# Who normalises images 9 to 11, and who makes the first expert input: moving work between VectorE and GpSimd in the last rounds

## The chip, the cores and the metric

One core of a Trainium2 chip. The metric is the device time of one execution in microseconds (us), the median over runs.

## The reference

Sixteen images of 128 channels and 32 x 32 pixels pass through one block:

```
x = x + conv_attention(layernorm_over_channels(x))     # k softmax over pixels, context k.v, out = context.q, 1x1 conv
t = tokens(x)                                          # 1024 pixels as tokens of 128 channels
n = (t - mean) / sqrt(var + eps)                       # over the channels
w = softmax(mean_over_images(n) @ Wr + br)             # 8 experts, one weight per pixel and expert
t = t + sum_e w[:, e] * expert_e(n)                    # three layers of 128, batch norm and relu after the first two
```

The routing weights need the mean of n over all 16 images, so every expert product's weighting comes after all the attention.

## The kernel before, in words

It has two phases. The first is 16 rounds (t = 0 to 15), one image each, software-pipelined: in round t, TensorE makes the k products of image t, turns e and adds the G products of image t, finishes the output of image t-1 (heads_out, the m product, add_m), turns x1 of image t-2 into tokens, and the other engines normalise the tokens of image t-3 and add them to a running sum `feat` for the routing. The second phase is 128 slots (16 images x 8 experts), three layers each. A few expert products are slipped into round 15 and the tail between the phases; the first is `half_layer1(p_k, 0, 0)` in round 15, made from `xs_hi[0]` and `xs_lo[0]`.

Every engine runs its own program in the order written; semaphores tie them. Rounds 0 to 3 and 12 to 15 are written out, 4 to 11 are two turns of a loop. What matters of each engine in rounds 12 to 15:

- TensorE: k products (`k_half`, L583), `heads_out` (L506), turn of x1 (L564), turn of a coming x (only up to round 12), in round 15 `half_layer1` (L627), the y product (L460), three turns of e (`turn_e`, L597), `add_m` (L515 to L517), G products (`add_g`, L609) with the fourth turn of e, `turn_rows` (L526).
- ScalarE: `gT` (L800), `move_rows` (L890), two exponentials (`exp_half`, L916), copy of the turned x1 (L814), `mT_hi` (L818), `move_e` 0 and 1 (L906), `high_part` (xn_hi, L861), `move_e` 2 and 3, and its own norm chunks of image t-3 (`norm2_high`, L868; four of eight for images from 9 on, two before).
- VectorE: head maxima (L1145, L1148), `y_sb` (L1039), `statistics` (L1129 to L1139), `mT_lo` (L1058), bn_stats (L1109), the x1 sum (L1067), `xn_lo` (L1071), and in rounds 12 to 14 `norm2_part` (L1117).
- GpSimd: `scale_x` (L1368), `statistics` (pow, L1344; shift, L1351), then `norm2` (L1358, L1360) and `add_feature` (L1432).
- SP issues the DMAs in the order written: the store of `rows_out` (L334), the load of the broadcast row that scale_x multiplies by (L348), x, x1 scratch, and `load_rows` (L327), which waits for `xs_made`.

The ties that the text uses: `scale_x` waits for the row load and for the statistics; `high_part` waits for `scale_x`; `norm2_high` and `norm2` wait for the shift (`ln_done`); the row load waits for the store, which waits for `move_rows`, which stands behind `norm2_high` on ScalarE; `add_feature` waits for both halves of the chunks.

The first expert input is image 0's x1, read back into `xs_in[0]`, multiplied by one broadcast row (`scale_xs`), shifted by another (`shift_xs`), cast to `xs_hi[0]` (`first_xs_high`), and the remainder is `xs_lo[0]` (`split_low`).

Of the kernel before, what the change touches and what calls it, by code (L numbers as in the profile page):

```python
# [26 lines left out]
ALU = mybir.AluOpType  # L27
# [3 lines left out]
IMAGES, C, SIDE = 16, 128, 32  # L31
PIXELS = SIDE * SIDE
# [24 lines left out]
def at(t, n):  # L57

    return isinstance(t, int) and t == n


def metaformer_kernel(nc, x, w_qkv, w_out, b_out, Wr, br, W1, W2, Wo, small, bo, ident_in, heads_in, out):
# [25 lines left out]
    with ExitStack() as ctx:  # L88
# [700 lines left out]
        def _(act):  # L789
# [4 lines left out]
            def step(t, r, s, n, a, c, f, d):  # L794
                p = r % 2
                q = 1 - p
                if c:
                    act.wait_ge(g_done, t)
                    wait(act, y_done, t - 1)
                    nc.scalar.copy(gT[:], p_g[:, 0:LATENT]).then_inc(g_moved, 1)  # L800
                    move_rows(t, p, p_e)
                exp_half(t, p, 0)
                if at(t, 0):
                    move_rows(0, 0, p_e)
                exp_half(t, p, 1)
                if at(t, 0):
                    move_by_head(1)
                    copy_x(2, 2)
                if f:
                    act.wait_ge(x1t_done, t - 1)  # L810
                    wait(act, norm2_last, t - 3)
                    if at(t, 3):
                        act.wait_ge(w_split, 1)
                    nc.scalar.copy(x1_tokens[p], p_chan.rearrange("p (n c) -> p n c", c=C)).then_inc(copy2_done, 1)  # L814
                if c:
                    act.wait_ge(m_done, t)
                    wait(act, mx_done, t - 1)
                    nc.scalar.copy(mT_hi[:], p_g[:, 256:384]).then_inc(m_hi_done, 1)  # L818
                move_e(t, r, 0)
                move_e(t, r, 1)  # L820
                if s and not at(t, 0):
                    copy_x(t + 3, (r + 3) % 4)
                if at(t, IMAGES - 2):
                    first_xs_high(0)
                if at(t, IMAGES - 1):
                    h1_high(0, 0, p_k)
                if a and not at(t, 0):
                    high_part(t, (r + 1) % 4, q)
                move_e(t, r, 2)
                if at(t, IMAGES - 1):  # L830
                    norm2_high(t - 3, r, x1_tokens[q], xn2T)
                move_e(t, r, 3)
                if at(t, IMAGES - 1):
                    act.wait_ge(x1t_done, IMAGES - 1)
                    act.wait_ge(norm2_first, IMAGES - 3)
                    act.wait_ge(norm2_last, IMAGES - 3)
                    nc.scalar.copy(x1T[:], p_chan.rearrange("p (n c) -> p n c", c=C)).then_inc(copy2_done, 1)
                if at(t, 0):
                    high_part(t, (r + 1) % 4, q)
                    copy_x(3, 3)  # L840
                    act.wait_ge(expert_w, 6 * 16)
                    expert_weights_high(2)
                if at(t, 1):
                    act.wait_ge(w1_shifted, 1)
                    expert_weights_high(0)
                if at(t, 2):
                    act.wait_ge(scaled, 2)
                    expert_weights_high(1)
                if d and not at(t, IMAGES - 1):
                    norm2_high(t - 3, r, x1_tokens[q], xn2T)  # L850
# [34 lines left out]
            def move_rows(index, q, bank):  # L885

                act.wait_ge(rows_turned, index + 1)
                if not isinstance(index, int) or index >= 2:
                    act.wait_ge(rows_stored[q], stored_count(index, q) - 16)
                nc.scalar.activation(rows_out[q][:], bank[0:3 * CHUNKS, 384:512], ACT.Identity,  # L890
                                     bias=row_bias[:, 0:1]).then_inc(rows_moved, 1)

            def first_xs_high(b):

                act.wait_ge(xs_made, b + 1)
                nc.scalar.copy(xs_hi[b][:], xs_in[b][:]).then_inc(xs_hi_done, 1)
# [126 lines left out]
        def _(dve):  # L1023
            flat = [w_raw[:, k].rearrange("p e h -> p (e h)") for k in range(3)]

            def step(t, r, s, n, a, c, f, d):
                p = r % 2
                q = 1 - p
                for j in range(2):
                    head_max(t, j)  # L1030
                if c:

                    dve.wait_ge(exp_done, 2 * t)
                    nc.vector.reciprocal(rsum[:], sums[q][:]).then_inc(rsum_done, 1)
                    dve.wait_ge(rsum_done, t)
                    dve.wait_ge(y_done, t)
                    wait(dve, m_done, t - 1)
                    for j in range(2):
                        ins = nc.vector.tensor_scalar(y_sb[:, j, :], p_g[:, 128 * j:128 * (j + 1)], rsum[:, j:j + 1], None, ALU.mult)  # L1039
                    ins.then_inc(y_moved, 1)  # L1040
                if at(t, 0):
                    centre(0, 2, 2)
                    scale_weights(0)
                    halves(0, x_tokens[2], 2)
                if at(t, 1):
                    scale_weights(1)
                if n or at(t, IMAGES - 2):
                    statistics(t, slice(0 if n else 1, 2 if d else 1))
                if at(t, 0):

                    dve.wait_ge(wo_t2_done, 1)
                    nc.vector.tensor_tensor(bo_full[:], p_g[0:EXPERTS, 256:384], bo_sb[:], ALU.add).then_inc(bo_full_done, 1)
                    dve.wait_ge(shift_done, 1)
                    dve.wait_ge(scaled, 1)
                    nc.vector.tensor_tensor(flat[0], flat[0], p_chan, ALU.add).then_inc(w1_shifted, 1)
                if c:
                    dve.wait_ge(m_hi_done, t)
                    nc.vector.tensor_tensor(mT_lo[:], p_g[:, 256:384], mT_hi[:].bitcast(F32), ALU.subtract).then_inc(m_lo_done, 1)  # L1058
                if at(t, IMAGES - 1):
                    statistics(t, OF_X1)  # L1060
                if f:
                    halves(1, x1_tokens[p], t - 2)
                if c:

                    dve.wait_ge(mx_done, t)
                    dve.wait_ge(res_loaded[q], 8 * t + (0 if q else 8))
                    nc.vector.scalar_tensor_tensor(out=x_res[q][:], in0=p_chan, scalar=bout_sb[:, 0:1], in1=x_res[q][:],  # L1067
                                                   op0=ALU.add, op1=ALU.add).then_inc(x1_done, 1)
                if a:
                    dve.wait_ge(xn_hi_done, t + 2)  # L1070
                    nc.vector.tensor_tensor(xn_lo[q][:], x_in[(r + 1) % 4], xn_hi[q][:].bitcast(F32), ALU.subtract).then_inc(xn_lo_done, 1)  # L1071
                if s:
                    halves(0, x_tokens[(r + 3) % 4], t + 3)
                if isinstance(t, int) and IMAGES - 4 <= t < IMAGES - 1:
                    norm2_part(t - 3, r, x1_tokens[q], xn2T, range(4, CHUNKS), norm2_last)
                if at(t, IMAGES - 1):
                    statistics(IMAGES, OF_X1)
                    h1_low(0, 0, p_k)
# [212 lines left out]
        def _(pool):  # L1291
# [105 lines left out]

            def step(t, r, s, n, a, c, f, d):
                q = 1 - r % 2
                if at(t, 1):  # L1400
                    low_part(2, 1)
                if at(t, 2):
                    low_part(0, 2)
                if at(t, 3):
                    low_part(1, 3)
                if a:

                    pool.wait_ge(var_done, t + 3)
                    scale_x(t, (r + 1) % 4)
                if n or d:  # L1410
                    statistics(t, r, slice(0 if n else 1, 2 if d else 1))
                if at(t, IMAGES - 4):
                    scale_xs(0, 0)
                if at(t, IMAGES - 3):
                    shift_xs(0, 0)
                if at(t, IMAGES - 2):

                    pool.wait_ge(xn_lo_done, IMAGES)
                    split_low(0, 0)
                if d:  # L1420
                    if not isinstance(t, int) or t - 3 < SHARED or at(t, IMAGES - 1):
                        norm2(t - 3, r, x1_tokens[q], xn2T, range(scalar_share(t - 3), CHUNKS))
                    if at(t, IMAGES - 1):
                        statistics(IMAGES, 0, OF_X1)
                    add_feature(t - 3, xn2T)
# [83 lines left out]
```

## Time and profile before

| | |
|---|---|
| median of 3 runs | 778.53 us (777.77 to 779.61) |
| profiled execution | 777.63 us, span 775.8 us |
| TensorE matmul busy | 758.4 us, 98% of the span |
| VectorE busy | 523.1 us, 67% |
| ScalarE busy | 446.9 us, 58% |
| GpSimd busy | 624.2 us, 80% |
| granted TensorE clock | full in every slice |

Busy shares are averages over both phases. Starts are counted from the span's start; the second phase runs from about 257.8 us.

### The profile page before, as it was taken

To read this page: it belongs to the slowest core of one execution; us is meant where nothing else is said; L and a number is where in the kernel's file an instruction comes from. 1 tells how busy PE (TensorE), PEld (TensorE's weight loads), DVE (VectorE), ACT (ScalarE), POOL (GpSimd) and SP (SyncE) were. 2 spreads that over 40 slices of the span, in tenths; PEclk is the share of its full clock that TensorE was granted. 3 is DMA by queue.
4 is the path that set the end of the run, shared out by engine and by line. 5 is a ranking of instruction groups with operands and counts; after the bars stand their busy time and mean duration, and the time that the engine had idled before them with its cause. 6 is when DMAs were issued, how large, how long until landed. Compare 5 with 4: busy or idle time off the path is not lost.

```text
span 775.8 us, 11887 instructions
## 1 busy us (share of the span) xinstructions
PE 758.4 (98%) x3871; PEld 621.3 (80%) x3871; DVE 523.1 (67%) x914; ACT 446.9 (58%) x633; POOL 624.2 (80%) x373
## 2 busy tenths in 40 slices
PE   7999999999999999999999999999999999999998
PEld 5788888887777788888888888888888888888886
DVE  6678888788977765666666565666656656666665
ACT  4677878777866655445455445544545554454553
POOL 6356888897776898888888888888888888888874
PEclk9999999999999999999999999999999999999999
DMA  7244545446330703213031130303303022130100
GB/s 226 109 166 161 186 148 190 151 175 219 126 121 32 272 25 112 81 55 135 0 135 69 67 135 0 135 33 102 130 5 135 27 108 90 45 135 1 54 28 28
DMA packets 27263, 80.59 MB, mean 104 GB/s; under 512 B 3120, under 2 KB 8152, under 8 KB 27232
## 3 DMA queue, kind: packets, MB, share of 16 engines
q1 hardware_dynamic: 27232, 80.20, 29.1%
q8 instruction: 17, 0.28, 0.2%
q14 instruction: 14, 0.11, 0.0%
HBM read 63.13 MB, written 17.06 MB: 103 GB/s over the span
## 4 chain that ended last, share of the span: by engine, by line
PE 68%; DVE 3%; POOL 2%; issue 1%; ACT 0%; POOLq 0%; DVEq 0%; ACTq 0%
PE psum L619 66%; DVE xn2T L1117 1%; POOL norms L1344 1%; POOL feat L1432 1%; DVE rawmax L1145 1%; PE psum L564 1%; DVE st L1109 0%; POOL route_all L1360 0%; POOLq L88 0%; POOL h_lo L1396 0%; PE psum L767 0%; PE psum L747 0%; DVE x_res L1067 0%; PE psum L597 0%; ACT h_hi L943 0%
## 5 line engine op out<-in xcount | busy, mean ns | idle before, releaser
L1155 DVE SCALAR_TENSOR_TENSOR h_lo<-psum,h_hi 128x1024 fp32r<-128x1024 f32 x128 | 156.7, 1224 | 191.7 <-ACT h_hi L924 191.5
L924 ACT ACTIVATE h_hi<-psum 128x1024 fp32r<-128x1024 f32 x128 | 131.7, 1029 | 237.7 <-PE psum L619 237.7
L1396 POOL TENSOR_TENSOR h_lo<-w_raw,h_hi 128x1024 fp32r<-128x1024 f32 x64 | 154.8, 2420 | 37.4 <-ACT h_hi L943 37.4
L619 PE MATMUL psum<-h_hi,w_hi 128*128 128x512 f32 x382 | 118.4, 391 | 1.9 <-ACT route_all L936 1.1
L1176 DVE SCALAR_TENSOR_TENSOR w_raw<-psum,minus_t,route_all 128x1024 f32<-128x1024 f32 x93 | 118.5, 1275 | 2.3 <-POOL h_lo L1396 2.3
L619 PE MATMUL psum<-h_lo,w_hi 128*128 128x512 f32 x382 | 119.0, 393 | 0.0
L619 PE MATMUL psum<-h_hi,w_lo 128*128 128x512 f32 x382 | 118.4, 391 | 0.0
L1396 POOL TENSOR_TENSOR xn_lo<-feat_most,xn_hi 128x1024 fp32r<-128x1024 f32 x31 | 74.6, 2407 | 34.2 <-ACT xn_hi L943 34.2
L619 PEld LDWEIGHTS psum<-h_hi,w_hi 128*128 128x128 f32 x382 | 71.4, 188 | 18.9 <-ACT route_all L936 1.3
L619 PEld LDWEIGHTS psum<-h_lo,w_hi 128*128 128x128 f32 x382 | 71.8, 188 | 15.6
L619 PEld LDWEIGHTS psum<-h_hi,w_lo 128*128 128x128 f32 x382 | 71.8, 188 | 15.2
L619 PE MATMUL psum<-xs_lo,w_hi 128*128 128x512 f32 x252 | 78.5, 393 | 0.0
L619 PE MATMUL psum<-xs_hi,w_hi 128*128 128x512 f32 x252 | 78.3, 392 | 0.0
L619 PE MATMUL psum<-xs_hi,w_lo 128*128 128x512 f32 x252 | 78.1, 391 | 0.0
L1396 POOL TENSOR_TENSOR xn_lo<-w_raw,xn_hi 128x1024 fp32r<-128x1024 f32 x32 | 77.1, 2411 | 1.1 <-ACT xn_hi L943 1.1
L943 ACT CAST h_hi<-w_raw 128x1024 fp32r<-128x1024 f32 x64 | 66.7, 1042 | 0.0
L619 PEld LDWEIGHTS psum<-xs_hi,w_hi 128*128 128x128 f32 x252 | 47.0, 188 | 11.4 <-issue 0.8
L619 PEld LDWEIGHTS psum<-xs_lo,w_hi 128*128 128x128 f32 x252 | 47.3, 188 | 10.3
L916 ACT ACTIVATE route_all<-psum,negmax 128x1024 f32<-128x1024 f32 x32 | 35.7, 1115 | 34.2 <-DVE negmax L1148 33.4
L619 PEld LDWEIGHTS psum<-xs_hi,w_lo 128*128 128x128 f32 x252 | 47.3, 188 | 10.0
L1344 POOL TENSOR_TENSOR norms<-terms,const 128x16 f32<-128x16 f32 (+1 forms) x21 | 48.7, 2318 | 7.6 <-DVE terms L1139 7.5
L906 ACT ACTIVATE route_all<-psum,norms 128x256 f32<-128x256 f32 x128 | 50.7, 489 | 2.6 <-PE psum L597 2.5
(224 smaller groups left out, 1444.6 us busy)
## 6 DMA issues: line engine op xcount, KB each, us to landing
rows<-rows_scratch SPq DMA_DIRECT2D x16, 1024.0 KB, 7.3
x_res<-in_x SPq DMA_DIRECT2D x16, 512.0 KB, 4.3
x_scratch<-x_res SPq DMA_DIRECT2D x16, 512.0 KB, 2.7
xs_in<-x_scratch SPq DMA_DIRECT2D x16, 512.0 KB, 4.9
x_res<-x_scratch SPq DMA_DIRECT2D x16, 512.0 KB, 3.3
out<-x_res SPq DMA_DIRECT2D x15, 512.0 KB, 2.6
w_raw<-rows_scratch SPq DMA_DIRECT2D x11, 512.0 KB, 3.7
z_early<-in_x SPq DMA_DIRECT2D x8, 512.0 KB, 3.9
```

The source lines that it names most:

```text
L564: mm = pe.transpose(dst[0:rows, 128 * n:128 * (n + 1)], chunk(n), ident[:])
L619: mm = pe.matmul(dst[:, px], w[:, which, e, :], part[:, px], start=first and w is w_hi and part is hi, stop=last and part is lo, skip_grou ...
L906: ins = nc.scalar.activation(ekT[:, chunk, :], e_out[i][:, LATENT * n:LATENT * (n + 1)], ACT.Identity, scale=norms[:, (r + 2) % 4, RSTD, 0 ...
L916: nc.scalar.activation(ek[j], k_out[j], ACT.Exp, bias=negmax[:, j:j + 1], accum_out=sums[p][:, j:j + 1]).then_inc(exp_done, 1)
L924: nc.scalar.activation(h1_hi[r][:], z1[r] if src is None else src, ACT.Relu).then_inc(h1_hi_done, 1)
L943: nc.scalar.copy(h2_hi[r][:], h2w[r]).then_inc(h2_hi_done, 1)
L1117: ins = nc.vector.tensor_scalar(out[:, n, :], tokens[:, n, :], norms[:, k, RSTD, 1, n:n + 1], norms[:, k, SHIFT, 1, n:n + 1], ALU.mult, AL ...
L1145: nc.vector.tensor_reduce(rawmax[:, j, n:n + 1], k_out[j][:, BANK * n:BANK * (n + 1)], AX.X, ALU.max).then_inc(max_done, 1)
L1155: nc.vector.scalar_tensor_tensor(out=h1_lo[r][:], in0=z1[r] if src is None else src, scalar=0.0, in1=h1_hi[r][:].bitcast(F32), op0=ALU.max ...
L1176: nc.vector.scalar_tensor_tensor(out=h2w[k % RING], in0=z, scalar=minus_t2[:, e:e + 1], in1=weights, op0=ALU.max, op1=ALU.mult).then_inc(h ...
L1344: ins = nc.gpsimd.tensor_tensor(norms[:, k, RSTD, ks], terms[:, VARIANCE, ks], const[:, MINUS_HALF].rearrange("p (k n) -> p k n", k=2)[:, ...
L1396: nc.gpsimd.tensor_tensor(h2_lo[r][:], h2w[r], h2_hi[r][:].bitcast(F32), ALU.subtract).then_inc(h2_lo_done, 1)
```

## The change

In rounds 12, 13 and 14 the four norm chunks 4 to 7 of images 9, 10 and 11 are made by GpSimd (`norm2`) instead of VectorE (`norm2_part`). The first expert input is scaled and shifted by VectorE at the end of rounds 13 and 14 instead of by GpSimd in rounds 12 and 13. ScalarE's cast of it moves from round 14 to round 15, ahead of the first exponential, and GpSimd's split from round 14 to the head of round 15.

```
 ScalarE, step:
                     move_rows(t, p, p_e)
+                if at(t, IMAGES - 1):
+                    first_xs_high(0)
                 exp_half(t, p, 0)
...
                     copy_x(t + 3, (r + 3) % 4)
-                if at(t, IMAGES - 2):
-                    first_xs_high(0)
                 if at(t, IMAGES - 1):
                     h1_high(0, 0, p_k)
 VectorE, step:
                 if s:
                     halves(0, x_tokens[(r + 3) % 4], t + 3)
-                if isinstance(t, int) and IMAGES - 4 <= t < IMAGES - 1:
-                    norm2_part(t - 3, r, x1_tokens[q], xn2T, range(4, CHUNKS), norm2_last)
+                if at(t, IMAGES - 3):
+
+                    dve.wait_ge(xs_loaded[0], 16)
+                    dve.wait_ge(rows_loaded, 16)
+                    nc.vector.tensor_tensor(xs_in[0][:], xs_in[0][:], rows[:, PIXELS:], ALU.mult).then_inc(xs_scaled, 1)
+                if at(t, IMAGES - 2):
+                    dve.wait_ge(xs_scaled, 1)
+                    nc.vector.tensor_tensor(xs_in[0][:], xs_in[0][:], rows[:, 0:PIXELS], ALU.add).then_inc(xs_made, 1)
 GpSimd, step:
                 q = 1 - r % 2
+                if at(t, IMAGES - 1):
+                    split_low(0, 0)
                 if at(t, 1):
...
                     statistics(t, r, slice(0 if n else 1, 2 if d else 1))
-                if at(t, IMAGES - 4):
-                    scale_xs(0, 0)
-                if at(t, IMAGES - 3):
-                    shift_xs(0, 0)
-                if at(t, IMAGES - 2):
-
-                    pool.wait_ge(xn_lo_done, IMAGES)
-                    split_low(0, 0)
                 if d:
-                    if not isinstance(t, int) or t - 3 < SHARED or at(t, IMAGES - 1):
-                        norm2(t - 3, r, x1_tokens[q], xn2T, range(scalar_share(t - 3), CHUNKS))
+                    norm2(t - 3, r, x1_tokens[q], xn2T, range(scalar_share(t - 3), CHUNKS))
```

## Rows read from the trace of the kernel before

**Rows 1.** Busy time by stretch, rounds 12 to 14: us, then busy (instructions) by engine.

```profile
172.98:185.53 12.55, 12.55 (x90) 10.50 (x88) 10.46 (x37) 9.59 (x20) 10.35 (x10) 1.00 0.71 251
185.53:199.17 13.64, 11.98 (x82) 9.71 (x80) 12.07 (x33) 9.97 (x23) 10.52 (x6) 1.00 0.34 120
199.17:212.63 13.46, 12.16 (x82) 9.72 (x80) 12.22 (x33) 10.75 (x24) 9.28 (x6) 1.00 0.39 125
```

**Rows 2.** The chain of waits, rounds 14 and 15: start us, us, what.

```profile
211.18 3.16 DVE xn2T L1117 x4
...
224.76 1.64 POOL norms L1344
```

**Rows 3.** Timeline of round 12, three engines: start us, us, instruction.

```profile
175.64 1.12 ACT L916 ACTIVATE route_all<-psum,negmax 128x1024 f32<-128x1024 f32 x1 [1.87 <-DVE negmax L1148]
...
177.15 0.61 DVE L1039 TENSOR_SCALAR y_sb<-psum,rsum 128x128 f32<-128x128 f32 x2
...
179.99 0.48 PE L515 MATMUL psum<-xn_hi,mT_hi 128*128 128x512 f32 x1
```

**Rows 4.** Timeline of GpSimd, rounds 13 to 15.

```profile
192.70 2.39 POOL L1368 TENSOR_TENSOR z_early<-z_early,w_raw 128x1024 f32<-128x1024 f32 x1 [2.06 <-DVE terms L1139]
195.04 2.91 POOL L1344 TENSOR_TENSOR norms<-terms,const 128x16 f32<-128x16 f32 x1
...
205.90 2.40 POOL L1368 TENSOR_TENSOR z_early<-z_early,w_raw 128x1024 f32<-128x1024 f32 x1 [1.96 <-DVE terms L1139]
208.25 1.65 POOL L1344 TENSOR_TENSOR norms<-terms,const 128x8 f32<-128x8 f32 x1
...
211.34 2.41 POOL L1390 TENSOR_TENSOR xs_lo<-xs_in,xs_hi 128x1024 fp32r<-128x1024 f32 x1 [1.16 <-DVE xn_lo L1071]
214.48 2.41 POOL L1432 TENSOR_TENSOR feat<-feat,xn2T 128x1024 f32<-128x1024 f32 x1 [0.73 <-issue]
...
222.93 1.74 POOL L1360 TENSOR_SCALAR xn2T<-x1T,norms 128x128 f32<-128x128 f32 x4
```

**Rows 5.** Timeline of ScalarE, round 13.

```profile
195.47 1.05 ACT L861 CAST xn_hi<-z_early 128x1024 fp32r<-128x1024 f32 x1 [0.66 <-PE psum L517]
196.43 1.56 ACT L906 ACTIVATE route_all<-psum,norms 128x256 f32<-128x256 f32 x4
198.27 1.65 ACT L868 ACTIVATE xn2T<-x1T,norms 128x128 f32<-128x128 f32 x4 [0.29 <-POOL norms L1351]
```

**Rows 6.** Row loads of rounds 13 and 14: issue (timeline), then landing time (DMA view).

```profile
188.51 0.34 SPq L348 DMA_DIRECT2D w_raw<-rows_scratch  x1
...
201.82 0.34 SPq L348 DMA_DIRECT2D w_raw<-rows_scratch  x1
...
w_raw<-rows_scratch SPq DMA_DIRECT2D x1, 512.0 KB, 3.4
...
w_raw<-rows_scratch SPq DMA_DIRECT2D x1, 512.0 KB, 3.9
```

**Rows 7.** Timeline of TensorE and VectorE, rounds 13 and 15.

```profile
191.81 0.71 PE L460 MATMUL psum<-y_sb,wqkv_sb 128*128 128x128 f32 x4 [1.66 <-DVE y_sb L1039]
...
196.52 2.79 PE L609 MATMUL psum<-route_all 128*128 128x256 f32 x12
...
217.08 0.50 PE L627 MATMUL psum<-xs_hi,w_hi 128*128 128x512 f32 x1
...
218.00 0.71 PE L460 MATMUL psum<-y_sb,wqkv_sb 128*128 128x128 f32 x4
...
222.19 1.28 DVE L1067 SCALAR_TENSOR_TENSOR x_res<-psum,bout_sb,x_res 128x1024 f32<-128x1024 f32 x1
```

**Rows 8.** Timeline of VectorE and GpSimd side by side, round 13 and tail.

```profile
196.62 1.22 DVE L1071 TENSOR_TENSOR xn_lo<-z_early,xn_hi 128x1024 fp32r<-128x1024 f32 x1
...
254.26 1.73 DVE L1176 SCALAR_TENSOR_TENSOR w_raw<-feat,minus_t,route_all 128x1024 f32<-128x1024 f32 x1 [0.54 <-ACT route_all L936]
255.19 3.02 POOL L1396 TENSOR_TENSOR h_lo<-w_raw,h_hi 128x1024 fp32r<-128x1024 f32 x1 [0.27 <-ACT h_hi L943]
```

## The prediction

> **What bounds the kernel now.** I read four views in this order. First the busy times by stretch, cut at the starts of the rounds (the first k matmul of a round; round 12 begins at 172.98). The change touches no instruction of the second phase, which waits for the first phase's end as a whole; so only rounds 12 to 15 and the tail behind them can move, and a shift there passes through to the end one to one. The reader is to see that round 12 takes 12.55 us with TensorE busy all the time, while rounds 13 and 14 take 13.64 and 13.46 with TensorE busy 11.98 and 12.16 [rows 1]. Second the chain of waits: through rounds 13 to 15 it passes through VectorE's norm chunks, then the head maxima, and after round 15 it lies on GpSimd (norms of round 16 at 224.76) [rows 2]. Third the timeline, engine by engine, with distances taken from the round's first matmul, called K. Fourth the DMA queue for the rows that scale_x waits for.
>
> In round 12 the second exponential's inputs are in time: y_sb at K + 4.17 and the first m matmul of add_m at K + 7.01 [rows 3]. In round 13 VectorE is still in its norm chunks when the k matmuls are done: the chunk group at 211.18 took 3.16 us [rows 2] for a piece of work that GpSimd does in 1.74 [rows 4], because GpSimd's scale, shift or split of the expert input ran beside it. y's product waited 1.66 us and came at K + 6.28 [rows 7].
>
> **What the change takes away.** Three groups of four chunks leave VectorE (rounds 12, 13, 14); GpSimd's scale_xs, shift_xs and the place of split_low leave its rounds 12 to 14, ScalarE's cast leaves round 14 (1.05 us by the cast of the same size, [rows 5]). GpSimd gets four chunks instead, 0.2 + 1.74 us a round for some 2.4 taken away [rows 4]: it gets no fuller. VectorE gets two tensor_tensor of 128x1024 with both inputs in SBUF; the nearest row, xn_lo, has 1.22 us [rows 8].
>
> Round 13, K = 185.53. Without the chunks VectorE reads the first maximum when it is made, y_sb is ready at K + 4.78 = 190.3 (K + 4.17 plus 0.61, [rows 3]) and, as no x is turned in this round, TensorE takes it about then: y at 190.4 for 191.81, a gain of 1.4. add_m, which waits for mT_lo, comes at about K + 6.75 = 192.3 (K + 7.01 less the 0.3 or so of the missing turn). From there to the end of a round it is 5.5 us (179.99 to 185.53, [rows 1, 3]), less a little: if nothing else were late, round 13 would end at 197.7. Something else is: scale_x of this round. Its input row load was issued at 188.51 and landed 3.4 us later, at 191.9 [rows 6], and the change moves neither (it hangs on ScalarE's own four chunks of round 12, then gT and the row move). So scale_x starts at 192.0 instead of 192.70 [rows 4], ends at 194.4, and the cast xn_hi starts there instead of at 195.47 [rows 5]. ScalarE has queued the third e move behind that cast: 0.95 for the cast, 0.8 for half of the four activations of 1.56 [rows 5], 196.2; then the last two quarters of the G products, 1.8 (three take 2.79, [rows 7]). K of round 14 is about 198.0, a gain of 1.15 us, not 1.4.
>
> Round 14. One ring sets its pace: scale_x, pow 2.91, shift 0.2; then ScalarE's chunks of image 10 (1.65), gT and the row move, the store, the load (issued at 201.82, 3.9 to land, [rows 5, 6]), scale_x again. Before, it ran from 192.70 to 205.90, 13.2 us [rows 4]: longer than round 12 took. This ring is the next thing late when VectorE's stall is gone. It starts 0.7 earlier. But the new multiply stands right behind xn_lo: xn_hi ends at 195.4, xn_lo 195.5 to 196.7, the multiply 196.65 to 197.85, and the pow ends at 197.3. What does the shift do beside a VectorE instruction with two SBUF inputs? The rows of the tail show holding: a VectorE instruction with two such inputs started at 254.26 and ended at 255.99, and GpSimd's next large one, started under it at 255.19, took 3.02 for the 2.4 of its size, so it was held for 0.6 [rows 8]. Bounds: no hold, 0; held to the multiply's end, 0.45 (0.35 to 0.5). I take 0.35. scale_x of round 14: 205.90 less 0.70, plus 0 to 0.5: 205.2 to 205.7, taken 205.55. Its cast starts at 207.95, the e move ends at 209.7, K of round 15 is 211.5 instead of 212.63: a gain of 1.1 us at that point.
>
> **What the change adds in round 15.** split_low now stands at the head of GpSimd's round 15, so behind add_feature of image 11, and half_layer1 on TensorE waits for it, where before it had long been done (split from 211.34 to 213.75, half layer at 217.08 = K + 4.45, no wait [rows 4, 7]). What follows GpSimd from scale_x at 205.55: end 207.9, pow of eight columns 1.65 to 209.55, then the shift; xn_lo runs 208.95 to 210.15, so the shift is held to 210.2 and ends at 210.4; four chunks to 212.4; add_feature, which also waits for ScalarE's chunks (third and fourth e moves to 210.5, then 1.65: 212.2), 212.5 to 214.9 (2.41 [rows 4]). VectorE's add begins after xn_lo or the shift and ends at 211.5 to 212.3, ScalarE has done gT and rows at 212.9, the cast 1.05 ends at 214.0: before the split, so it is hidden, and before the first exponential, due at K + 2.66 = 214.15 [rows 3]; cover 0.15 us, and each us of the cast beyond it is a us on both exponentials. Split 2.4: xs_lo done at 217.3. TensorE is there at K + 4.45 = 215.95 and waits 1.35 us. The whole gain of rounds 13 and 14 is used up by this wait.
>
> What is queued behind it: y, m and the e turns. y comes 0.97 after, 218.3 for 218.00 [rows 7]; the e turns start at 218.8 for 218.55; mT_lo is no later than before, because ScalarE's exponentials and the copy ahead of mT_hi come about 1 us earlier in this round. The x1 sum of round 15 waits for add_m: 222.3 for 222.19 [rows 7]. From there on statistics, GpSimd's norms at 224.76 [rows 2] and the tail follow unchanged in order. Sum: rounds 13 and 14 -1.1, wait of half_layer1 +1.35, less the 0.15 of slack in front of add_m and the shift of ScalarE: +0.1 by the x1 sum (222.3 for 222.19), and without the two holds (0.35 and 0.5) -0.4 to -0.6. SP: load_rows(1) now waits for VectorE's add (211.5 to 212.3); behind it in SP's queue stands the store of round 15's rows, which waits for ScalarE until about 212.9 anyway, and the loads behind that one are wanted much later. The two inputs of the multiply were there in round 12 already, when GpSimd used them: no wait.
>
> I take the middle, -0.1 us, against the profiled execution (777.63 us, span 775.8): 777.5; the median of the runs shown is 0.9 higher, 778.53, so 778.4.
>
> The Trainium skill ("SBUF — State Buffer", section "Who interferes with whom") says that a VectorE instruction with two SBUF inputs and a GpSimd instruction that reads SBUF exclude one another for the whole of the one that comes first. Rows of the tail agree; but xn_lo at 196.62 took its usual 1.22 inside a pow of 2.91 that had begun at 195.04 [rows 4, 8], so the trace does not show it for the pow. Were it so, every xn_lo would end about 1.2 us later than its row; the rule in full is what rival B rests on.
>
> **Rivals.**
> A, the forecast: what VectorE gives back is eaten by the GpSimd chain in front of half_layer1; -0.5 to +0.5 us. Chance 0.60.
> B, slower: the add of round 14 stands back to back behind xn_lo, VectorE keeps the port, and the shift comes only after the add, at 211.3 instead of 210.2. Then ScalarE's chunks start at 211.55, add_feature at 213.55, the split ends at 218.35, y comes at 219.35 and the x1 sum at 223.3: +1.1 us, 779.6. It passes 0.2% only if xs_lo is done after about 218.7, i.e. with another 0.35 of hold (the four chunks beside the add, or ScalarE's cast pushed behind 214.15 so that the exponentials slip too: +1.6 to +2). Against it: GpSimd is asking already when xn_lo ends. Chance 0.22, a good half of it within 0.2%.
> C, faster: the wait of half_layer1 is short, because the load lands faster or the ring of scale_x is not held, and the gain of 1.1 at K of round 15 survives: 777.3. To pass 0.2% (1.56 us) the ring would have to turn in less than 12.5 us; the end of that road is TensorE's own busy time, 11.98 and 12.16 for 13.64 and 13.46 [rows 1]: -3.0 us, 775.4. For it: the loads landed between 3.4 and 3.9. Against it: five serial steps of GpSimd and ScalarE of known length. Chance 0.18, a good half within 0.2%.
>
> **Numbers.** 0.2% is 1.56 us, about what a measurement can tell from no change here (the runs shown lie between 777.77 and 779.61). Same: 0.60 + 0.13 + 0.09 less 0.05 for the scatter of the medians = 0.77. Slower 0.13, faster 0.10. The range takes in B's +1.1 and C's -1.1 and the scatter: 777.0 to 780.1.
>
> **What would show it.** Round 13 about 1.1 us shorter and the wait for y_sb nearly gone; round 14 no shorter than round 13 was cut, with scale_x at 205.2 to 205.9; a new wait of 0.9 to 1.9 us of TensorE for xs_lo in round 15; ScalarE's cast ending before the first exponential is due; norms of round 16 at 224.4 to 225.2. I am wrong if the split starts before 214 (then C) or after 215.7 (then B), or if the shift of round 14 starts after 211.

## The result, and the profile after

The changed kernel takes 781.13 us (median of 19 runs, 778.48 to 782.72) against 778.53 of the kernel before in the same sessions: ratio 1.0024, 95% interval 1.0016 to 1.0032. By the ratio it is slower by about 1.9 us (0.24%), by the medians by 2.6, and it scatters over 4.2 us where the kernel before scatters over 2.5. The profiled execution took 779.51 us with a span of 777.3 (before: 777.63 and 775.8).

Busy time by stretch, rounds 12 to 15 of the kernel after (they begin at 172.9, 185.6, 198.6 and 212.2):

```profile
185.62:198.60 12.98, 12.23 (x82) 9.71 (x80) 10.13 (x29) 9.24 (x21) 9.76 (x9) 1.00 0.36 125
198.60:212.17 13.57, 12.23 (x81) 9.71 (x80) 9.90 (x28) 10.64 (x25) 10.13 (x11) 1.00 0.34 118
212.17:228.10 15.93, 14.05 (x95) 11.68 (x93) 10.17 (x37) 11.96 (x24) 12.09 (x16) 1.00 0.49 166
```

Against [rows 1] round 13 gained 0.66 us, round 14 lost 0.1 (13.57 for 13.46), and round 15 lost 1.8 (it took 14.16 before). GpSimd in rounds 13 to 15:

```profile
192.49 2.38 POOL L1374 TENSOR_TENSOR z_early<-z_early,w_raw 128x1024 f32<-128x1024 f32 x1 [2.93 <-issue]
194.83 2.91 POOL L1350 TENSOR_TENSOR norms<-terms,const 128x16 f32<-128x16 f32 x1
197.82 0.58 POOL L1357 TENSOR_TENSOR norms<-terms,norms 128x8 f32<-128x8 f32 x1
...
206.07 2.38 POOL L1374 TENSOR_TENSOR z_early<-z_early,w_raw 128x1024 f32<-128x1024 f32 x1 [3.15 <-ACT route_all L906]
208.40 1.65 POOL L1350 TENSOR_TENSOR norms<-terms,const 128x8 f32<-128x8 f32 x1
210.13 0.71 POOL L1357 TENSOR_TENSOR norms<-terms,norms 128x8 f32<-128x8 f32 x1
210.92 1.05 POOL L1364 TENSOR_TENSOR ln_wait<-const 128x8 f32<-128x8 f32 x1
211.96 1.73 POOL L1366 TENSOR_SCALAR xn2T<-w_raw,norms 128x128 f32<-128x128 f32 x4
213.83 2.39 POOL L1431 TENSOR_TENSOR feat<-feat,xn2T 128x1024 f32<-128x1024 f32 x1
216.17 2.36 POOL L1396 TENSOR_TENSOR xs_lo<-xs_in,xs_hi 128x1024 fp32r<-128x1024 f32 x1
```

The reader is to see three stretched rows: the two shifts (L1357, 0.58 and 0.71 us for 0.20) and ln_wait (L1364, 1.05 for 0.20), each under one of these VectorE instructions with two SBUF inputs:

```profile
197.12 1.22 DVE L1078 TENSOR_TENSOR xs_in<-xs_in,rows 128x1024 f32<-128x1024 f32 x1
...
209.55 1.22 DVE L1071 TENSOR_TENSOR xn_lo<-z_early,xn_hi 128x1024 fp32r<-128x1024 f32 x1 [1.23 <-ACT xn_hi L861]
210.70 1.22 DVE L1081 TENSOR_TENSOR xs_in<-xs_in,rows 128x1024 f32<-128x1024 f32 x1
```

Behind them four chunks, add_feature and the split run back to back, and TensorE waits for the last of them. TensorE's waits in rounds 13 to 15 (answers to [rows 7]):

```profile
190.46 0.71 PE L460 MATMUL psum<-y_sb,wqkv_sb 128*128 128x128 f32 x4 [0.21 <-DVE y_sb L1039]
...
196.74 1.99 PE L609 MATMUL psum<-route_all 128*128 128x256 f32 x8 [0.54 <-ACT route_all L906]
...
210.31 1.99 PE L609 MATMUL psum<-route_all,xs_in 128*128 128x256 f32 x8 [1.15 <-ACT route_all L906]
...
218.68 0.47 PE L627 MATMUL psum<-xs_hi,w_hi 128*128 128x512 f32 x1 [1.88 <-POOL xs_lo L1396]
```

The 1.66 us in front of y in round 13 (and 1.30 in round 14) are gone but for 0.2, and come back as 0.54 and 1.15 for ScalarE's e moves, which stand behind scale_x, and 1.88 for xs_lo. The chain of waits, which ran over VectorE's chunks before [rows 2], now begins at the four chunks right behind the held ln_wait and runs over the split:

```profile
211.97 1.72 POOL xn2T L1366 x4
...
216.17 2.37 POOL xs_lo L1396
...
218.68 0.94 PE psum L627 x3
...
225.94 1.64 POOL norms L1350
```

GpSimd's norms of round 16 start at 225.94 for 224.76, and the first bias product of the second phase comes 1.4 us later than before. As a measure that does not hang on where a run stands in the prologue I use D from here on: from the last `turn_rows` of round 12 to the x1 sum of round 15. Before: 222.19 - 185.50 = 36.69 us; after: 223.51 - 185.59 = 37.92.

The two profiled executions differ by 1.9 us: 1.5 in the span and 0.4 outside it. The medians differ by 2.6; what is missing is in no row of this execution, and a second one shows it.

### The profile page after: what moved, and what is told of

Same layout as the page of the kernel before. It is cut to its first block, busy times and chain, and to the rows that moved or that the text cites. A ratio compares the mean times of both kernels' runs of the same rounds, so it can differ in the third digit from the quotient of the medians.

```text
span 777.3 us, 11889 instructions
## 1 busy us (share of the span) xinstructions
PE 760.4 (98%) x3871; PEld 622.8 (80%) x3871; DVE 517.0 (67%) x904; ACT 446.9 (58%) x633; POOL 626.7 (81%) x386
## 4 chain that ended last, share of the span: by engine, by line
PE 68%; POOL 3%; issue 1%; DVE 1%; POOLq 0%; ACT 0%; DVEq 0%; ACTq 0%
PE psum L619 66%; POOL feat L1431 1%; POOL norms L1350 1%; PE psum L564 1%; POOL route_all L1366 0%; POOLq L88 0%; POOL h_lo L1402 0%; POOL xs_lo L1396 0%; PE psum L767 0%; PE psum L747 0%; POOL xn2T L1366 0%; PE psum L627 0%; DVE st L1115 0%; PE psum L597 0%; ACT h_hi L943 0%
```

## The experiments

Each ratio is to the kernel before on the same chip, with its 95% interval. The kernel before has a median of 778.58 us on the chip of a to d, 777.86 on that of e, g, h and i, and 777.89 on that of j to m; so times of different groups are compared by their ratios, not as they stand. D is from one profiled execution each.

**a_again**: the changed kernel unaltered.

> The changed kernel once more, for the granted clock of its runs beside those of the kernel before. Theory 1 (only the wait of half_layer1 for xs_lo costs): profiled span 777.0 to 777.6, and time over the kernel before about 1.5 to 1.9 us wherever both run at full clock; slower runs are those with a granted clock below 1. Theory 2 (TensorE's longer idle stretches in rounds 14 and 15 lower its clock): runs with a clock of 0.998 and less are common here and absent in the kernel before, and a profile with such a clock shows the low stretch right behind round 14 or 15. Theory 3 (a cost outside the traced span): time less span is 2.2 us here against 1.8 before in all runs.

780.73 us, ratio 1.0030 (1.0021 to 1.0040), span of the profiled execution 778.7. This profile caught what the other lacked. Busy time by stretch, with the granted TensorE clock as the third number from the end:

```profile
216.00:218.00 2.00, 0.85 (x8) 0.61 (x6) 0.92 (x5) 1.76 (x4) 2.00 (x2) 1.00 1.02 318
218.00:219.00 1.00, 0.26 (x1) 0.29 (x2) 0.00 (x0) 0.41 (x1) 0.59 (x1) 1.00 1.01 242
219.00:220.00 1.00, 1.00 (x8) 0.88 (x8) 0.00 (x0) 0.00 (x0) 0.00 (x0) 1.00 0.78 299
220.00:221.00 1.00, 1.00 (x8) 1.00 (x7) 0.54 (x4) 0.48 (x2) 0.00 (x0) 0.61 0.30 107
221.00:222.00 1.00, 1.00 (x6) 1.00 (x5) 0.95 (x7) 0.99 (x3) 0.39 (x1) 0.50 0.00 0
222.00:223.00 1.00, 1.00 (x5) 0.90 (x4) 1.00 (x6) 0.48 (x2) 1.00 (x1) 0.50 0.00 0
223.00:224.00 1.00, 1.00 (x4) 0.76 (x4) 0.09 (x1) 0.23 (x1) 0.84 (x4) 0.69 0.00 0
```

TensorE was idle for 1.2 us in round 14 and 1.9 in round 15, and 1.5 us after that wait had ended the clock went to half, 1.2 GHz of 2.4, for some 3.4 us. The e turns took 2.51 us for 1.47, and from the half product to the x1 sum it is 6.44 us for 4.83: the dip costs 1.6 us. (D is 39.68, 1.8 more; 0.15 of it was there before the half product.) Of the 29 timed runs of the changed kernel 21 lie above 780 us. The mean granted clock of a run fits: the seven runs at 1.00 lie at 778.5 to 779.8, and all 21 above 780 have 0.993 to 0.998 (3.4 us at half speed are 0.2% of the span). It does not say where the low stretch is. 24 of 32 runs of the kernel before have less than 1.00 too, at a median of 778.62 for 778.04, and the remaining run of the changed kernel, the profiled one of 779.51 with 0.998, has it near the start:

```profile
8.00:12.00 4.00, 2.51 (x11) 1.88 (x12) 2.73 (x12) 1.51 (x5) 3.69 (x7) 0.71 1.04 300
12.00:16.00 4.00, 3.67 (x19) 3.11 (x18) 3.71 (x11) 3.17 (x7) 2.29 (x7) 0.86 1.11 341
```

So theory 2 was wrong in that low clocks are not absent in the kernel before. Time less span is 2.2 us in every run here, 1.8 in the kernel before, as theory 3 said.

**b_split_late**: the kernel before with one part of the change.

```
 GpSimd, step:
+                if at(t, IMAGES - 1):
+                    split_low(0, 0)
...
-                if at(t, IMAGES - 2):
-
-                    pool.wait_ge(xn_lo_done, IMAGES)
-                    split_low(0, 0)
```

> The kernel before with one part of the change alone: split_low of the first expert input at the head of GpSimd's round 15. Theory 1: xs_lo is done at about 219.3 (add_feature ends at 216.9, split 2.4), TensorE waits 2.2 us in round 15 and the tail is 2.2 us later: about +2.2 us, i.e. more than the whole change costs in its profile (+1.5), because the change also gains some 0.5 to 1 us in rounds 13 and 14. Rival (rounds 13 and 14 or the holds between the engines lose the time, the place of the split does not matter): within 0.5 us of the kernel before.

778.61 us, ratio 1.0003 (0.9994 to 1.0012), D = 37.24. The expectation was wrong in its numbers: add_feature no longer waits behind the split, so it came forward, xs_lo was ready after a wait of 0.66 us and not 2.2, and D lost 0.55. The place of the split alone costs little (nothing that the time shows); it needs the longer GpSimd chain in front of it.

**c_half_later**: takes the wait away from y and the e turns.

```
 TensorE, step, round 15:
-                if at(t, IMAGES - 1):
-                    pe.wait_ge(exp_done, 2 * t + 1)
-                    pe.wait_ge(xs_lo_done, 1)
-                    half_layer1(p_k, 0, 0)
...
                 turn_e(t, 2)
                 if at(t, IMAGES - 1):
+                    pe.wait_ge(exp_done, 2 * t + 1)
+                    pe.wait_ge(xs_lo_done, 1)
+                    half_layer1(p_k, 0, 0)
                     half_layer1(p_k, 0, 1).then_inc(l1_done, 1)
```

> The changed kernel with the first half of the early layer-1 product moved behind the three e turns of round 15, where the second half stands, so that y and the e turns no longer wait for xs_lo. Theory 1: y at K + 4.9 of round 15 = 217.0, e turns at 217.5; the half product waits for xs_lo at 218.5 some 0 to 0.3 us only; the x1 sum of round 15 comes at 221.9 to 222.3 instead of 223.5: 1.2 to 1.6 us faster than the changed kernel, about -0.2 to +0.3 against the kernel before. Rival (the tail hangs on the GpSimd chain and not on that wait): less than 0.5 us gained.

778.72 us, ratio 0.9998 (0.9988 to 1.0007), D = 36.20: 1.7 us less than the changed kernel in D and 2.0 in the median. y comes as soon as y_sb is ready:

```profile
218.25 0.71 PE L456 MATMUL psum<-y_sb,wqkv_sb 128*128 128x128 f32 x4 [0.20 <-DVE y_sb L1038]
```

No run lies above 779.0, so the high runs are gone with the wait. The wait of half_layer1 carried the loss.

**d_add_early**: the multiply and the add of VectorE stand ahead of `xn_lo` instead of behind it, same lines.

> The changed kernel with VectorE's multiply and add put ahead of xn_lo, where VectorE is idle (0.6 us in round 13, 1.2 us in round 14), so that they end before GpSimd's shift and ln_wait. Theory of the holds: the shift of round 13 goes back from 0.58 to 0.20 us, scale_x of round 14 starts 0.2 to 0.4 earlier, shift 0.2 to 0.7 and ln_wait 0.2 instead of 1.05, xs_lo is done 1.1 to 1.5 us earlier and the time is 0.9 to 1.4 us less than the changed kernel's. Rival (the holds are not what sets the split): below 0.4 us; xn_lo of round 13, pushed back by the multiply, may give 0.3 us back at the start of round 14.

778.79 us, ratio 1.0004 (0.9995 to 1.0013), D = 36.90:

```profile
198.09 0.20 POOL L1357 TENSOR_TENSOR norms<-terms,norms 128x8 f32<-128x8 f32 x1
...
209.91 1.02 POOL L1357 TENSOR_TENSOR norms<-terms,norms 128x8 f32<-128x8 f32 x1
211.00 0.20 POOL L1364 TENSOR_TENSOR ln_wait<-const 128x8 f32<-128x8 f32 x1
```

The shift of round 13 and ln_wait are free again; the shift of round 14 is still held, by xn_lo now. xs_lo is done 1.0 us earlier after round 12, and D follows with 1.0: 0.4 from the shift of round 13 through the ring, 0.5 from the holds of round 14, and 0.1 because the row load landed sooner. The wait for xs_lo is down to 1.34 us and the one in round 14 to 0.65; what they still cost is about what rounds 13 and 14 gain against the kernel before. The time fell by more than D, 1.9 us in the median for 0.9 to 1.4 expected, and no run lies above 780: the high runs are gone here too, although a wait of 1.34 us is left.

**e_both**: c and d together.

> The changed kernel with both mends together: half_layer1 behind the e turns of round 15, and VectorE's multiply and add ahead of xn_lo. If the wait in round 15 is the whole loss (theory 1), the second mend adds little to the first, since nothing waits for xs_lo any more: within 0.3 us of c_half_later, 778.4 to 778.8. If the held shift and ln_wait also delay ScalarE's chunks, gT and the row move (theory of the holds), it is 0.3 to 0.8 us faster than c_half_later.

777.27 us, ratio 0.9996 (0.9987 to 1.0005), D = 35.43. This does not decide between the two expectations. D is 0.77 less than in c_half_later, but the row load of round 14 landed in 3.5 us here and in 4.2 there, and that alone is 0.7; scale_x of round 13, which the difference between the two does not touch, came 0.3 later into its round here. The hold that is gone from the ring is the 0.38 us of round 13's shift. By the ratios the two kernels differ by 0.2 us, inside the intervals.

**g_fill**: the wait of round 15 filled with work. Its seven extra matmuls compute nothing that is used.

```
                 if at(t, IMAGES - 1):
                     pe.wait_ge(exp_done, 2 * t + 1)
+                    for _ in range(7):
+                        pe.matmul(p_k[:, BANK:PIXELS], wkT_hi[:, 0:128], xn_hi[p][:, 0:BANK], start=True, stop=True)
                     pe.wait_ge(xs_lo_done, 1)
                     half_layer1(p_k, 0, 0)
```

> The changed kernel with seven extra matmuls of 512 columns (some 1.65 us) into a free PSUM bank where TensorE waits 1.9 us for xs_lo in round 15; the wait itself stays, and the results of the seven are not used. Theory 2 (the idle stretch lowers the granted clock in most executions, which costs another 1.5 us): the low stretch at 220 to 224 is gone, the median falls from 780.7 to 779.2 to 779.7 and the scatter shrinks. Theory 1 alone (only the wait counts): no change, 780.7, or a little slower.

779.1 us, ratio 1.0014 (1.0005 to 1.0023), no run above 779.67 (11 runs). TensorE still has to wait for xs_lo, only busy:

```profile
216.69 1.87 PE L455 MATMUL psum<-xn_hi,wkT_hi 128*128 128x512 f32 x7
218.77 0.51 PE L629 MATMUL psum<-xs_hi,w_hi 128*128 128x512 f32 x1 [0.21 <-POOL xs_lo L1398]
```

No stretch of this profile has a granted clock below 1.00. Useless work made the kernel faster by 0.8 to 1.2 us by the ratios (1.0014 for 1.0024 and 1.0030), and the runs spread over 1.3 us for the 4.2 of the changed kernel. That is the clock's part of the loss. (D is 37.32, 0.6 less than in the changed kernel's profile, because the row loads landed in 3.5 and 3.6 us for 3.8 and 4.0; that is the luck of one execution and not the edit.)

**m_fill14**: four such matmuls in round 14 instead (ahead of `add_g(t, r, 2)`), the wait of round 15 open.

> The changed kernel with four extra matmuls of 512 columns in round 14, where TensorE waits 1.15 us for the third e move; results not used. The wait of 1.9 us in round 15 stays open. If the granted clock falls because of the two idle stretches together (some 3 us within 10 us), the low stretch behind round 15 goes as with g_fill: median 779.2 to 779.7 against 780.7. If the wait of round 15 alone does it: the runs with a low clock stay in the majority, 780.5 to 781.

779.26 us, ratio 1.0023 (1.0013 to 1.0034), 5 of 12 runs above 780, TensorE waiting 1.72 us for xs_lo. Between the two expectations: fewer high runs than the changed kernel (21 of 29), more than g_fill (none of 11). The idle time of round 14 seems to count as well; 12 runs do not settle its share, and its ratio is that of the changed kernel. This chip reads 0.7 us lower, but the gap between 779.29 and 780.03 in these runs leaves the count as it is.

**h_xs_only**: multiply and add on VectorE, cast and split late, but the chunks stay on VectorE.

```
 to the changed kernel, VectorE:
+                if isinstance(t, int) and IMAGES - 4 <= t < IMAGES - 1:
+                    norm2_part(t - 3, r, x1_tokens[q], xn2T, range(4, CHUNKS), norm2_last)
                 if at(t, IMAGES - 3):
...
 GpSimd:
                 if d:
+                    if not isinstance(t, int) or t - 3 < SHARED or at(t, IMAGES - 1):
                         norm2(t - 3, r, x1_tokens[q], xn2T, range(scalar_share(t - 3), CHUNKS))
```

> One half of the change alone: multiply and add on VectorE, cast and split in round 15, but the norm chunks stay on VectorE (ahead of the multiply and the add). GpSimd is then nearly empty in rounds 12 to 14: VectorE's chunks take 1.1 us a round instead of 2.5 to 3.2 since no large GpSimd instruction runs beside them. Theory 1 (the GpSimd chain in front of the split): the chain loses four chunks and the held ln_wait, 1.9 to 2.8 us, but add_feature still waits for both halves of the chunks: xs_lo at K + 5 to 6, a wait of 0.5 to 1.5 us, time 778.3 to 779.5. Rival (what costs is VectorE working for the expert input at all): as slow as the changed kernel, 780.5.

777.26 us, ratio 0.9988 (0.9979 to 0.9997), D = 36.10. VectorE's chunks, 3.16 us in [rows 2], beside an idle GpSimd:

```profile
210.02 1.11 DVE L1125 TENSOR_SCALAR xn2T<-w_raw,norms 128x128 f32<-128x128 f32 x4
```

Faster than both kernels, and faster than expected (778.3 to 779.5; 0.7 us of that is the chip), with a wait of 1.06 us for xs_lo still in it:

```profile
217.00 0.47 PE L627 MATMUL psum<-xs_hi,w_hi 128*128 128x512 f32 x1 [1.06 <-POOL xs_lo L1398]
```

**i_norm_only**: the chunks on GpSimd, the expert input as before (scale_xs, shift_xs and split_low at their old places).

> The other half alone: the norm chunks of images 9 to 11 on GpSimd, the expert input made by GpSimd as before (scale in round 12, shift in 13, split in 14). Theory 1: GpSimd has just room (scale_xs, four chunks and add_feature end at 191.7, scale_x is due at 192.0), VectorE's stalls of 1.3 to 1.7 us in front of y are gone, no hold on the shift, no wait in round 15: the 0.6 to 1.1 us gained in rounds 13 and 14 stay, 777.5 to 778.0. Rival (GpSimd becomes the bound): scale_x late by up to 1 us in each of three rounds, 779 to 781.

776.72 us, ratio 0.9983 (0.9974 to 0.9992), D = 35.48. GpSimd did not become the bound:

```profile
203.41 2.37 POOL L1429 TENSOR_TENSOR feat<-feat,xn2T 128x1024 f32<-128x1024 f32 x1
206.61 2.39 POOL L1366 TENSOR_TENSOR z_early<-z_early,w_raw 128x1024 f32<-128x1024 f32 x1 [0.83 <-DVE terms L1137]
```

It had 0.83 us left in front of scale_x, although it did all of both jobs, and TensorE did not wait for xs_lo. So either half of the change gains, and the two together lose.

**j_xs_later**: h with c's edit.

> h_xs_only (norm chunks on VectorE, multiply and add on VectorE, cast and split in round 15) with half_layer1 behind the e turns. h_xs_only still waited 1.06 us for xs_lo. Theory 1: that wait goes, the x1 sum of round 15 comes at K of round 13 + 35.1 to 35.5 instead of + 36.1: 0.6 to 1.0 us less than h_xs_only, ratio to the kernel before 0.9975 to 0.998. Rival (the tail is set elsewhere by now): the same as h_xs_only.

776.36 us, ratio 0.9977 (0.9968 to 0.9986), D = 35.38: 0.7 less than h, as theory 1 says. The fastest version by its ratio, 1.5 us below the kernel before in the median (1.8 by the ratio).

**k_xs_early_later**: j with the multiply and the add ahead of xn_lo.

> As j_xs_later, with the multiply and the add ahead of xn_lo. In h_xs_only they held add_feature (2.77 and 2.79 us for 2.39). Theory of the holds: those go, but xn_lo is pushed back by up to 0.6 us in round 13 and 14; with half_layer1 out of the way nothing waits for add_feature or the split, so no more than 0.2 us either way against j_xs_later.

776.07 us, ratio 0.9979 (0.9971 to 0.9988), D = 35.05: not to be told from j by time.

**l_norm_later**: i with c's edit, the control.

> i_norm_only (norm chunks on GpSimd, expert input on GpSimd as before) with half_layer1 behind the e turns. There TensorE did not wait for xs_lo, but the half product stood ahead of y, 0.8 us, while y_sb was ready. So y can come up to 0.5 us earlier: 0.0 to 0.4 us less than i_norm_only. This is the control for the mend: if the mend alone were worth 1 us or more without any wait there, it would not be the wait that it took away in c_half_later.

777.04 us, ratio 0.9995 (0.9986 to 1.0004), D = 35.72. Slower than i_norm_only and not 0.0 to 0.4 faster as expected: 0.24 us in D, 0.9 by the ratios, whose intervals overlap. Where TensorE does not wait for xs_lo, the edit gives nothing. What it gave in c and j was the wait.

## Why the prediction was wrong, point by point

The text forecast no change, 778.4 with 777.0 to 780.1; 781.13 lies outside. (The middle of its two sums, +0.1 and -0.4 to -0.6, is -0.2 and not the -0.1 it took; that decides nothing.) The mechanism of case A was there: the wait of half_layer1 for xs_lo ate the gain. Its size was off, because a hold in the GpSimd chain and 0.5 us of the ring were missing, and one mechanism, the clock, was missing altogether.

- **Round 13**: the wait for y_sb went as forecast (y at 190.46, forecast 190.4), and the ring took part of the gain as forecast. scale_x came at 192.49 for 192.0, since the load was issued 0.1 later and landed in 3.8 us and not 3.4. Round 14 began at 198.6, forecast 198.0.
- **The hold of the multiply**, forecast 0.35 us: 0.38 (0.58 for 0.20). Right.
- **Round 14**: scale_x at 206.07, forecast 205.55, above the range of 205.2 to 205.7. The turn of the ring was right (13.58 us, forecast 13.55); the 0.5 is what scale_x of round 13 was late, and the prediction had taken its load from one landing time. Such loads landed in 3.4 to 4.2 us in the profiles of these kernels. Round 15 began at 212.2 for 211.5: a gain of 0.5, not of 1.1.
- **Who takes the port behind xn_lo**: "the shift is held to 210.2 and ends at 210.4", before the add. Right: the shift began at 210.13 and ended at 210.84, well before the end of the add (210.70 to 211.92). But the sentence went on "four chunks to 212.4", which has room for the usual 0.20 us of ln_wait, the small instruction between, and none for a hold. It fell under the add, which the prediction itself let run to 211.5 or later, and was held 0.85 us. This is the term of the sum that was mis-sized: a hold was priced for the shift and not for the next instruction in line. With it and the 0.5 of the ring xs_lo was done at 218.5, forecast 217.3, and TensorE waited 1.88 us, forecast 1.35. The sign that the text had given for B came (the split after 215.7; it started at 216.17), and B's timetable fits closely (split to 218.35, x1 sum at 223.3), but not for B's reason: the shift did not wait for the add. That B's number fits D is luck.
- **The cast on ScalarE**: hidden, as forecast (213.97 before an exponential that began at 214.83).
- **What the wait costs**: forecast x1 sum at 222.3, +0.1 by D's end; measured 223.5, D +1.2. From xs_lo to the x1 sum it is 5.0 us in both, so the whole of that miss is xs_lo. "mT_lo is no later than before" did not hold (220.39 for 219.57: ScalarE waited 1.72 us for y's product, which stands behind the half product), but nothing waited for it: TensorE worked without a break from the half product at 218.68 to add_m at 221.91 and on.
- **The clock**: not in the prediction at all. It counted TensorE's waits as costing their own length. In a_again the dip cost 1.6 us, and g_fill, without it, took 0.8 to 1.2 off by the ratios. It forecast one idle stretch of 1.35 us where two of 1.15 and 1.88 came; that they might have a price of their own was not asked.
- **0.4 us outside the span**: the forecast was added up inside the span and carried to the median by a constant. What passes outside the span was not the same (2.2 us for 1.8). No row of the kernel before could show this.

Summed: +1.2 in D, +0.4 outside the span, and the clock's 1.6 in some seven executions of ten, is 2.8 on average; measured are 1.9 and 2.3 by the two ratios (2.6 and 2.2 by the medians). The three terms explain the whole and somewhat more; that every run above 780 had the dip behind round 15 is inferred, from one profile, from the mean clocks and from c, d and g, which have no such run; it was not seen in each.

## What to carry to other kernels

When two engines can each hold the other off SBUF, price the hold for every instruction in line, the tiny ones too, not just for the one whose wait you looked for. Ask of a freed engine where the step that it pulled behind it now stands: each half of this change gained (0.9 and 1.3 us by its ratio) and the two together lost, because both lengthened one serial chain in front of one wait (none in i, 1.06 us in h, 1.88 with both). A wait of TensorE of some 2 us can cost more than its length; let the work that does not need the late operand go first.

## What the runs showed of the hardware that was not expected

- GpSimd instructions of 0.20 us took 0.58, 0.71 and 1.05 us when they began under a VectorE tensor_tensor with two SBUF inputs, and were back at 0.20 when it was moved (d_add_early). This agrees with the Trainium skill ("SBUF — State Buffer", section "Who interferes with whom"): whichever comes first holds the shared port, and the shape of the other does not matter. It does not agree for the pow, which by that rule should have held xn_lo and again did not (1.22 us at 209.55, begun inside 208.40 to 210.05).
- Between two such VectorE instructions back to back, GpSimd, which was asking already, got in: the shift ended 0.14 us after the second one began by the records. It got one instruction in, and the next was held. The profiles of a, c, g and m repeat it (shift 0.71 to 0.72, ln_wait 1.06).
- After idle stretches of 1.2 and 1.9 us, TensorE's granted clock fell from 2.4 to 1.2 GHz while it was busy again, 1.5 us after the wait had ended, and stayed there for some 3.4 us; in another execution of the same kernel it did not. Seven useless matmuls in the gap kept all 11 runs within 1.9 us of the median of the kernel before; those of the changed kernel go up to 4.2 above it.
- Time outside the span was 2.2 us for all kernels that carry both halves of the change (changed kernel, a, c, d, e, g, m) and 1.8 for all others (before, b, h, i, j, k, l): 2.18 to 2.29 and 1.75 to 1.85 in every run. The cause stays open.
